# Two softmax attentions in one fused kernel: the block of value products is moved ahead in every slot of TensorE's order

## The reference, cut to what matters

```python
xn = layernorm(x)
x = x + memory(xn) + ffn0(xn)          # ffn0: conv -> attention -> 8 experts
xn = layernorm(x)
x = x + attn1(xn) + routed_experts(xn)

# attention of ffn0: 16 heads of 8 columns, every key seen
attn = softmax(einsum('bhqd,bhkd->bhqk', q, k) / sqrt(8))
ctx = einsum('bhqk,bhkd->bhqd', attn, v)

# attn1: the same with a causal mask, then a convolution makes new queries
ctx = causal_attn(q, k, v)
q2 = conv(ctx)
ctx2 = causal_attn(q2, k, v)           # same keys and values
out = ctx2 @ out_w.T + out_b
```

## Time and profile before

| | |
|---|---|
| median of three runs | 3540.61 us |
| profiled execution, first to last instruction | 3517.1 us |
| TensorE busy | 3224.9 us, 92% |
| VectorE busy | 2570.7 us, 73% |
| ScalarE busy | 2069.9 us, 59% |
| layer 0's attention, stretch 440 to 1150 us: PE, DVE, ACT busy | 654.28, 595.37, 536.56 of 710 us |
| layer 1's attentions, stretch 2400 to 3440 us: PE, DVE, ACT busy | 984.00, 802.85, 729.50 of 1040 us |

### The profile page before, as it was taken

How to read it: one execution, slowest core, us unless ns; L and a number is a source line. 1 busy time by engine, 2 the same in 40 slices (tenths; PEclk the granted TensorE clock), 3 DMA queues, 4 the chain that set the end, 5 groups by cost and what they waited for, 6 DMA issues and landing times. The chain is left out here.

```text
span 3517.1 us, 77360 instructions
## 1 busy us (share of the span) xinstructions
PE 3224.9 (92%) x30347; PEld 1872.0 (53%) x30347; DVE 2570.7 (73%) x5088; ACT 2069.9 (59%) x4201; POOL 830.8 (24%) x756
## 2 busy tenths in 40 slices
PE   6887699999999899999999999889999999999998
PEld 6876222222222377777777777645555444444454
DVE  5876788888888456776776766777777777777774
ACT  6774277777777543443434434337667767777766
POOL 3321111110110223323323423223333121111110
PEclk9998699999999999999999999979999999999999
DMA  4100211111110100110110110122222121112111
GB/s 141 30 13 1 62 46 55 55 39 54 46 52 28 33 22 23 33 35 23 33 35 23 33 35 23 47 71 61 61 61 48 48 66 48 46 44 53 42 27 29
DMA packets 180473, 151.89 MB, mean 43 GB/s; under 512 B 44388, under 2 KB 160900, under 8 KB 179972
## 3 DMA queue, kind: packets, MB, share of 16 engines
q1 hardware_dynamic: 173092, 141.21, 14.2%
q0 software_dynamic: 6144, 4.72, 1.0%
q10 hardware_dynamic: 864, 0.79, 0.1%
HBM read 48.45 MB, written 32.65 MB: 23 GB/s over the span
## 5 line engine op out<-in xcount | busy, mean ns | idle before, releaser
L1426 DVE TENSOR_REDUCE b_maxima<-psum 128x2 f32<-128x1024 f32 (+3 forms) x768 | 773.5, 1044 | 222.7 <-PE psum L1260 213.9
L1366 ACT ACTIVATE b_prob<-psum 128x512 f32<-128x512 f32 (+2 forms) x1536 | 725.4, 526 | 318.5 <-PE psum L1293 306.7
L1426 DVE TENSOR_REDUCE c_maxima<-psum 128x2 f32<-128x1024 f32 x512 | 602.5, 1221 | 117.7 <-PE psum L1254 116.6
L1366 ACT ACTIVATE c_prob<-psum 128x512 f32<-128x512 f32 x1024 | 535.9, 602 | 194.4 <-PE psum L1286 194.3
L2178 PEld LDWEIGHTS psum<-consts_layer,a_hid 128*128 128x128 f32 x4096 | 476.2, 192 | 53.6 <-issue 53.3
L2168 PE MATMUL psum<-a_x1t,consts_layer 128*128 128x512 f32 x1024 | 463.7, 598 | 16.0 <-issue 10.5
L2178 PE MATMUL psum<-consts_layer,a_hid 128*128 128x128 f32 x4096 | 477.8, 274 | 0.0
L2238 ACT ACTIVATE a_hid<-psum,consts_layer 128x512 f32<-128x512 f32 x512 | 347.7, 687 | 210.4 <-PE psum L2168 204.3
L1286 PE MATMUL psum<-b_qa,b_ka 64*128 64x512 bf16 (+3 forms) x2048 | 360.5, 303 | 54.5 <-ACT b_prob L1366 51.9
L1308 PE MATMUL psum<-b_prob,b_v 128*32 128x512 f32 (+3 forms) x4096 | 386.3, 449 | 0.3
L2400 DVE SCALAR_TENSOR_TENSOR a_acc<-psum,a_gprob,a_acc 128x128 f32<-128x128 f32 x512 | 143.7, 343 | 269.9 <-PE psum L2178 257.3
(11 more groups left out here) (406 smaller groups left out, 4319.5 us busy)
## 6 DMA issues: line engine op xcount, KB each, us to landing
b_qa<-b_part SPq DMA_DIRECT2D x192, 128.0 KB
c_qa<-c_part SPq DMA_DIRECT2D x96, 128.0 KB, 2.4
b_ka<-b_part SPq DMA_DIRECT2D x96, 128.0 KB
c_ka<-c_part SPq DMA_DIRECT2D x90, 128.0 KB, 2.4
consts_layer<-layer_in SPq DMA_DIRECT2D x1, 5419.0 KB, 19.3
c_xt<-xnt SPq DMA_DIRECT2D x17, 256.0 KB, 2.8
m_xin<-x SPq DMA_DIRECT2D x16, 256.0 KB, 4.2
xnt<-m_xt SPq DMA_DIRECT2D x16, 256.0 KB, 2.8
```

The lines of the kernel that those rows point to most:

```text
L1366: self.nc.scalar.activation(out, src, ACT.Exp, scale=SCALE).then_inc(self.s.free, 1)
L1426: self.nc.vector.reduce_max(out, src, X).then_inc(self.m.free, 1)
```

## The change

The block of value products moves: it stands directly behind maxima A, ahead of the S jobs, scores B and the M jobs. The order of a slot becomes: scores A, maxima A, values of the slot before, S jobs, scores B, M jobs, maxima B. Both branches of `if self.causal` are the same, and `half` is never given, so each block is still one group of four products. Lists of the other engines, the plan of the rings and every semaphore's count stay as they are.

```diff
@@ tensor_values
-    def tensor_values(self, pe, p, s):
+    def tensor_values(self, pe, p, s, half=None):
...
+        if half != 1:
+            pe.wait_ge(self.s.free, self.s.count("exp", p, s, self.heads(s, self.units(s)[-1])[-1]))
...
@@ tensor_turn
-            if self.has(p):
-                self.tensor_scores(pe, p, s, 0)
-            if self.has(p + 1):
-                self.tensor_maxima(pe, p + 1, s, 0)
-            if s == WHOLE and self.has(p - 1):
-                self.tensor_whole(pe, p - 1)
-            extra_s(p, s)
-            if self.has(p) and len(units) > 1:
-                self.tensor_scores(pe, p, s, 1)
-            for job in self.moved(p, s):
-                self.tensor_shift(pe, *job)
-            for job in self.ended(p, s):
-                self.tensor_context(pe, *job)
-            extra_m(p, s)
-            if s and self.has(p):
-                self.tensor_values(pe, p, s - 1)
-            if s == 0 and self.has(p - 1):
-                self.tensor_values(pe, p - 1, SLOTS - 1)
-            if self.has(p + 1) and len(units) > 1:
-                self.tensor_maxima(pe, p + 1, s, 1)
+            def values(slots, half=None):
+                q, r = divmod(p * SLOTS + s - slots, SLOTS)
+                if self.has(q):
+                    self.tensor_values(pe, q, r, half)
...
+                scores(0)
+                maxima(0)
+                values(1)
+                on_s()
+                scores(1)
+                on_m()
+                maxima(1)
```

More of the change, by code:

```diff
@@ L1295, in tensor_scores @@
                             last.then_inc(self.s.ready, 1)
-    def tensor_values(self, pe, p, s):
+    def tensor_values(self, pe, p, s, half=None):
         nc, (g, t) = self.nc, divmod(s, T)
-        pe.wait_ge(self.s.free, self.s.count("exp", p, s, self.heads(s, self.units(s)[-1])[-1]))
-        if s == 0:
-            pe.wait_ge(self.m.free, self.m.count("v", self.turns[p].batch))
         pair, odd = divmod(g, 2)
-        if t == 0 and odd == 0:
-            pe.wait_ge(self.c_copied, p * PAIRS + pair)
-        q0 = t * P if self.causal else 0
+        first, last = odd == 0 and t == 0, odd == 1 and t == T - 1
+        if first and half is not None:
+            if half == 0:
+                return
+            half = None
+        if half != 1:
+            pe.wait_ge(self.s.free, self.s.count("exp", p, s, self.heads(s, self.units(s)[-1])[-1]))
+            if s == 0:
+                pe.wait_ge(self.m.free, self.m.count("v", self.turns[p].batch))
+            if first:
+                pe.wait_ge(self.c_copied, p * PAIRS + pair)
+        q0, q1 = t * P if self.causal else 0, S
+        if half is not None:
+            middle = (q0 + q1) // 2
+            q0, q1 = (q0, middle) if half == 0 else (middle, q1)
         for j in range(HG):
             column = GAP + (pair * 2 * HG + 2 * j + odd) * 32 - GAP * odd
-            last = nc.tensor.matmul(self.acc[32 * j:32 * (j + 1), q0:S], self.values(p)[:, t, column:column + 32],
-                                    self.prob[:, s % 2, j, q0:S], start=odd == 0 and t == 0, stop=odd == 1 and t == T - 1)
-        last.then_inc(self.pv_ready, 1)
+            product = nc.tensor.matmul(self.acc[32 * j:32 * (j + 1), q0:q1], self.values(p)[:, t, column:column + 32],
+                                       self.prob[:, s % 2, j, q0:q1], start=first, stop=last and half != 0)
+        if half != 0:
+            product.then_inc(self.pv_ready, 1)
     def tensor_context(self, pe, p, pair):
@@ L1329, in tensor_turn, with scores, maxima, on_s @@
         for s in range(SLOTS):
[L1330 to L1350 removed]
+            t = s % T
+            def scores(u):
+                if self.has(p) and u in self.units(s):
+                    self.tensor_scores(pe, p, s, u)
+            def maxima(u):
+                if self.has(p + 1) and u in self.units(s):
+                    self.tensor_maxima(pe, p + 1, s, u)
+            def values(slots, half=None):
+                q, r = divmod(p * SLOTS + s - slots, SLOTS)
+                if self.has(q):
+                    self.tensor_values(pe, q, r, half)
+            def on_s():
+                if s == WHOLE and self.has(p - 1):
+                    self.tensor_whole(pe, p - 1)
+                extra_s(p, s)
+            def on_m():
+                for job in self.moved(p, s):
+                    self.tensor_shift(pe, *job)
+                for job in self.ended(p, s):
+                    self.tensor_context(pe, *job)
+                extra_m(p, s)
+            if self.causal:
+                scores(0)
[5 more added lines that the diff above has]
+                maxima(1)
+            else:
+                scores(0)
+                maxima(0)
+                values(1)
+                on_s()
+                scores(1)
+                on_m()
+                maxima(1)
     def scalar_exponentials(self, act, p, s, u):
```

## The result

The changed kernel took 3585.58 us (median of four runs, 3583.13 to 3587.25) beside 3539.44 us for the kernel before, timed with it: ratio 1.0131, 95% interval 1.0116 to 1.0145. It is slower, by 46 us, and the forecast was 3640, 100 us slower. The direction was right and the size was more than twice the truth; the range, 3600 to 3676, missed.

The account below looks back on a forecast made before the run. The prediction took a loop through TensorE and ScalarE as the bound. Layer 0's +55 us and layer 1's +45 summed to +100, from 3540.6 to about 3640 us, range 3600 to 3676.

Parts of the forecast that it names:

- 1.3 a turn: Layer 1: added time from S jobs, contexts and a shift's saving, over 32 turns +42 us.
- The bound and the plain slot: Layer 0: a loop through TensorE and ScalarE sets the slot; without jobs it stays within 0.05, taken as 2.66 us.
- S jobs: Layer 0: jobs ahead of scores B lose their cover; additions 1.50 twice, 0.92, and 1.28 twice.
- Bank 7 and M jobs: Layer 0: the copy adds 1.0 us a turn, two contexts 1.08, `v` 0.91, shifts 0.
- I take 52.4: Layer 0: chosen turn length in us, between the sum 52.0 and 52.8 with leads and a late VectorE.
- and 16 turns: Layer 0: the 3.45 us more per turn was applied to every turn, giving +55 us.
- The term of 6.48: Layer 0: total us a turn added by the five S jobs: convolutions, `whole`, queries and keys.
- The falling clock: Rival, both attention stages: new stands bring 1.2 GHz for a tenth of the time, 3815 us; chance 0.02.
- The loop that is longer everywhere: Rival, both layers: each waiting block of values pays 0.2 to 0.3, +60 on top, 3700 us; chance 0.06.
- Nothing changes: Rival, whole kernel: TensorE, 92% busy with the same work, might be the bound throughout, 3541 us; chance 0.03.
- It gets faster: Rival, both layers: M jobs go for nothing and S jobs stay cheap, 3445 us; chance 0.05.
- The 23.5 us: Whole kernel: time taken to lie around the span, added to span 3617 for a median of about 3640.

Follow-up runs that it names:

- `c_s_late`: Against the kernel before: layer 0 alone has values behind maxima A, except the five slots with S jobs; 3505.6 us, ratio 0.9967.
- `b_late`: Against the kernel before: new order only in layer 1's turns 9 to 31, which have no experts; 3522.39 against 3513.95 us, ratio 1.0024.
- `before_again`: The kernel before, profiled once more without an edit; span 3514.6 us, run time 3516.38 us.
- `after_again`: The changed kernel, unedited, timed again against the kernel before; 3572.16 against 3516.54 us, ratio 1.0162.
- `c_between`: Against the kernel before: in all slots of layer 0 alone, values behind the S jobs and ahead of scores B; 3561.05 against 3539.12 us, ratio 1.0062.
- `c_only`: Against the kernel before: new order in layer 0 alone, old order in layer 1; 3547.05 against 3513.95 us, ratio 1.0090.
- `best`: Kernel before with values behind maxima A except in slots with S jobs, context jobs or copy of bank 7, both layers; 3514.09 against 3539.12 us, ratio 0.9927.
- `b_s_late`: Against the kernel before: layer 1 alone has the new order, except slots holding an S job in that turn; 3526.2 us, ratio 0.9963.

## Why the prediction was right in direction and wrong in size

In one sentence: the mechanism of layer 0 was right, but its price of 3.45 us was put on all 16 turns although two of them hold next to no S jobs, and was itself 0.96 too high; in layer 1 the term "1.3 a turn" was 0.52, because what the moved M jobs give back was left out.

**The bound and the plain slot.** Right. The loop through both engines sets the slot, and it has the length of the sum: 2.61 against 2.62 to 2.71, taken as 2.66. But the path isn't quite the one described. The prediction let the values wait for the second exponential of unit B and 0.06 more. The rows after show ScalarE starting at 766.91, 0.42 behind scores B; its first exponential ends 0.60 later, and 0.06 behind that the second half of the next scores A takes that bank at 767.57. Maxima A and the values follow in order, 0.53 later. That is 1.00 + 0.42 + 0.60 + 0.06 + 0.53 = 2.61. The prediction expected its "wait that is not there now" in front of the values; in plain slots the wait stands in front of scores A, and of the values of layer 0 the page shows 16.9 us of idle time, nearly all for the copy of bank 7.

**S jobs.** Right, and shown: the convolution was put at 2.66 + 1.50 = 4.16, and measured 4.15; queries and keys 3.94, measured 3.92. `whole` was put at 2.66 + 0.92 = 3.58, and measured 3.37. The term took the 1.39 from the start of the job to the first exponential from a slot in which ScalarE worked without a pause, from the exponentials of unit A to those of unit B at 727.22, so it held ScalarE's own time and not only the path through the job:

```profile
725.77 1.08 ACT L1366 ACTIVATE c_prob<-psum 128x512 f32<-128x512 f32 x2 [0.47 <-PE psum L1286]
726.74 0.60 ACT L1745 ACTIVATE c_ctxt<-psum 128x512 f32<-128x512 f32 x1
```

Now ScalarE starts at 792.76, 1.18 after the job's start at 791.58. `c_s_late` takes this term away and the loss turns into a gain. Only the cover was less than said: the stand in front of the second half of scores B is the 0.69 less the 0.22 by which the two halves follow each other anyway, 0.47. No term of the sum used it.

**Bank 7 and M jobs.** Right to 0.03, between blocks of values: slot 0 was put at 4.65 and measured 4.68, the context 3.20 and 3.20, `v` (805.38 to 801.79 below) 3.57 and 3.59. TensorE after; the maxima that precede the values wait for the copy-out of `v`:

```profile
801.79 1.07 PE L1317 MATMUL psum<-c_prob,c_v 128*32 128x512 f32 x8
...
805.06 0.39 PE L1254 MATMUL psum<-c_ka,c_qa 62*128 62x512 bf16 x2 [0.25 <-DVE c_v L1492]
805.38 1.06 PE L1317 MATMUL psum<-c_prob,c_v 128*32 128x512 f32 x8
```

**The sum of layer 0: two terms were mis-sized.** First the step "I take 52.4". A middle turn is 51.44. Of the 0.96 too much, 0.4 is what was added on the sum of the rows for leads and "a late VectorE", which aren't there; most of the rest is the plain slot taken at 2.66 (0.05 in each of five slots) and `whole` (0.2). Over 13 middle turns that is 12 us. Second the step "and 16 turns". The turns at the ends of the stage don't pay: turn 0 grew by 49.93 - 49.2 = 0.7 (it differs by as much between profiles of one order), turn 14 went from 45.07 to 44.76, and turn 15 from 50.37 to 48.19. For the last two the kernel says why: convolution, queries and keys in turn `p` are those of batch `p + 2`, so turns 14 and 15 hold none of them, and `whole` is their only S job. The term of 6.48 has nothing to act on there, and what the moved M jobs give back is left. With 2.5 for each of the 13 middle turns this makes 32.5 + 0.7 - 0.3 - 2.2 = 30.7; the stage grew from 780.9 to 811.7 us, from its first exponential to the end of its last. Had the three end turns paid 3.45 each as forecast, it would be 12 us more.

**Layer 1: the sum left out what the change gives back.** In the turns without experts the slots with two of the S jobs grew by 0.35 and 0.30 to 0.36, as forecast (0.36). `whole` cost 0.06 instead of the 0.3 taken, the contexts 0.13 each instead of 0.25. And three terms were missing: the slot of `v` became shorter by 0.36, the output product's two slots by 0.17 net, and slots 12 and 13 by 0.16. The turns of the two kinds grew by 0.26 and 0.78, not by 1.3. That gives 23 x 0.52 = 12 us by the middle turns, and 8.4 by the time of `b_late`, beside 29.9. The profiles show where the two part: against `before_again` turns 9 to 30 of `b_late` grew by 11.5 us together, and the last turn fell from 33.5 to 30.0. With the old order the last turn lies anywhere between 31.0 and 35.4 us, so how much of that is the change stays open. The prediction had seen that M jobs leave the loop, and credited it only to the shift, and in part to the contexts.

**TensorE's busy time.** It was to stay, and idle time to grow by some 100 us. Between the pages of `before_again` and `after_again` the busy time grew from 3219.4 to 3239.2 us, and the idle time, span less busy time, by 34 us.

**The rivals.** The falling clock is refuted: 1.00 in both windows after, and in the middle turns of layer 0 in each run here. The Trainium skill, "TensorE: Matmul & The Clock Gate", section "A second HAM failure mode: psum-queue depth-cycling", warns of clock swings in a kernel whose TensorE often idles for a moment while it cycles through PSUM banks. Here TensorE stands for 0.25 us in each plain slot of layer 0 and for up to 0.46 in others, and the trace doesn't agree with the rule. The loop that is longer everywhere is refuted for layer 0 by 2.61, and for layer 1 by turns that grew less than forecast. "Nothing changes" falls with the interval of the ratio. "It gets faster" was wrong for this kernel, and its mechanism was partly right: early values gain in most slots where no S job stands, which is what `c_s_late` and `best` use.

**The 23.5 us.** They were no part of the program's start or end, which is 1.8 us. The profiled execution of the earlier trace rows itself took 3518.93 us, 1.8 over its span, so it was faster than the three runs beside it; the chips of the last heading differ by as much. Added to the forecast, the 23.5 did no harm, since the changed kernel was timed where the one before took 3539.44.

**46 or 55.6 us.** The change costs 46 us (1.0131, 1.0116 to 1.0145) where it was timed first and 55.6 (1.0162, 1.0144 to 1.0180) where it was timed again. The intervals all but touch, and the profiles say where the gap would lie. Layer 0's stage grew by the same 30.8 and 30.9 us. The turns 9 to 31 of layer 1 take 821.6 and 823.1 us in the two profiles of the changed kernel, and 813.7 and 814.3 in `before_again` and `c_between`, where they have the old order. The nine turns with experts take 379.0 us in `after_again` against 368.3 in `before_again`, 10.7 more. In the first profile of the changed kernel they take 397.0; the only profile of the old order in which they are slow in the same way, `c_between`, has 392.2, and that is 4.8 less. So the change seems to cost less where these turns are slow anyway. It is one profile each, of different chips, and the cause stays open. For the same reason `c_between` (beside 3539.12) and `c_only` (beside 3513.95) are compared by their differences, with that much doubt.

## What to carry to other kernels

Where an engine works through a fixed list, place a block by what is queued behind it. A job whose time was hidden in a wait must keep that wait: a block of 1.00 us in front of the scores that feed ScalarE made a slot longer by 0.20 to 0.95 us where a job stood there too, and made the other eleven slots of a turn shorter by 1.0 together. Decide it slot by slot: here one order in all slots lost 1.3 to 1.6% and the choice by slot won 0.7%, with the same instructions. When summing such a change over turns, look which turns hold the jobs that pay, and take the turns at the ends by themselves, and write down the gains of the moved work with the same care as its losses.

## What the runs showed of the hardware that was not expected

The kernel before took 3513.95 and 3516.54 us in two groups of runs and 3539.12 and 3539.44 in two others; three of the groups are on one chip each, and for the fourth (3539.44) the chip isn't known. The difference of some 24 us lies nearly all in one place, the turns of layer 1 that hold the experts: turns 0 to 7 add up to 329.1 us in `before_again` and to 352.6 in `c_between`, whose layer 1 is the old one, while the middle turns after them have equal lengths (34.83 and 36.31). In the other six profiles in which these turns have the old order, all from the two chips with the shorter time, they add up to 328.2 to 330.6 us, whatever layer 0's order. The windows, `before_again` first:

```profile
2322.00:2690.00 368.00, 347.86 (x5146) 190.42 (x5142) 290.35 (x376) 254.88 (x563) 131.49 (x136) 0.98 0.29 63
```

and `c_between`:

```profile
2344.00:2735.00 391.00, 360.16 (x5126) 197.12 (x5124) 290.21 (x375) 253.76 (x561) 131.28 (x136) 0.95 0.27 59
```

VectorE, ScalarE and GpSimd have the same busy time. TensorE needs 12 us more for the same work at a granted clock of 0.95 instead of 0.98, and stands for 31 instead of 20 us. TensorE's waits in that stretch of `c_between` (total us, times, longest):

```profile
PE psum L1286 <- ACT b_prob L1399: 11.3, 32, 2.2
...
PE psum L1260 <- issue: 2.8, 3, 1.2
```

In `before_again` the wait for ScalarE is 6.3 us at most 0.3 each, and no stand without a releaser appears. Stands of up to 1.2 us for which the profile shows nothing are new there; `best` and `b_s_late`, from the same chip, have them too. The clock alone isn't the difference: in the first profile of the changed kernel these turns are slow as well (355.9 us against 337.9 in `after_again`), and its granted clock there is 0.98. What causes the stands stays open. It matters for method: a profile from one chip and a median from another differ by 0.7% with nothing changed, so a time is compared with its partner on the same chip only.
